# One delta-rule layer of a small transformer on one core: two activation-table switches per stage, a decay mask carried by unused partitions, and another order of the work

## The reference

```python
q = silu(x @ Wq); k = l2norm(silu(x @ Wk)); v = silu(x @ Wv)      # 16 heads of 16
log_f = log_sigmoid(x @ Wf)
gamma = -sigmoid(x @ Wgamma)
a = k * gamma[..., None] * exp(log_f)[..., None]
def step(S, inp):                       # over the 38 tokens of an image
    Sp = S * exp(gk)[..., None]
    u = einsum('bhk,bhkv->bhv', a, Sp) + v
    S = Sp + einsum('bhk,bhv->bhkv', k, u)
    return S, einsum('bhk,bhkv->bhv', q, S)
out = layer_norm(out * sigmoid(x @ Wg1 @ Wg2)) * norm_w @ Wo
```

## Time and profile before

| | us |
|---|---|
| median of 3 runs | 1996.59 (1990.41 to 1997.77) |
| the profiled execution | 1989.77 |
| its span | 1988.0 |
| the stage "ln2" | 21.7 (1281.40 to 1303.05) |
| k = 0, 1, 2 | 18.3, 26.8, 44.2 |
| k = 3 to 7, full | 58.8, 61.7, 58.5, 58.1, 58.1 |
| k = 8, 9, 10 | 56.5, 45.7, 29.7 |

### The profile page before, as it was taken

The page is one execution under the profiler, slowest core; times in us unless marked ns, Lnnn a source line. Parts: engine busy times, 40 slices in busy tenths (PEclk is TensorE's granted clock), DMA queues, the critical chain, the costliest instruction groups (busy, mean ns, idle before and its releaser), DMA issues. The chain is left out here.

```text
span 1988.0 us, 51796 instructions
## 1 busy us (share of the span) xinstructions
PE 1708.2 (86%) x22689; PEld 1517.3 (76%) x22689; DVE 1108.5 (56%) x2379; ACT 656.6 (33%) x1347; POOL 314.5 (16%) x284
## 2 busy tenths in 40 slices
PE   4677786799999999999999999876888888757589
PEld 4466675579988999989999999745877777756468
DVE  3655555674545555455555465566445555543885
ACT  3334534433322233232223232163333333223142
...
DMA packets 10070, 36.01 MB, mean 18 GB/s; under 512 B 3056, under 2 KB 6152, under 8 KB 7304
## 3 DMA queue, kind: packets, MB, share of 16 engines
...
...
## 5 line engine op out<-in xcount | busy, mean ns | idle before, releaser
L1042 ACT ACTIVATE hidden<-bank,moe_b 128x512 f32<-128x512 f32 (+1 forms) x320 | 213.3, 668 | 537.1 <-PE bank L934 524.5
L951 PE MATMUL bank<-moe_w2h,hidden_hi 128*128 128x256 f32 x1216 | 345.7, 284 | 0.0
L951 PE MATMUL bank<-moe_w2l,hidden_hi 128*128 128x256 f32 x1216 | 344.0, 283 | 0.0
L951 PE MATMUL bank<-moe_w2h,hidden_lo 128*128 128x256 f32 x1216 | 343.9, 283 | 0.0
L934 PE MATMUL bank<-x_hi,moe_w1h 128*128 128x512 f32 (+1 forms) x640 | 243.8, 381 | 2.9 <-ACT hidden L1042 2.8
L934 PE MATMUL bank<-x_lo,moe_w1h 128*128 128x512 f32 (+1 forms) x640 | 242.5, 379 | 0.0
L934 PE MATMUL bank<-x_hi,moe_w1l 128*128 128x512 f32 (+1 forms) x640 | 242.0, 378 | 0.0
L951 PEld LDWEIGHTS bank<-moe_w2h,hidden_hi 128*128 128x128 f32 x1216 | 233.1, 192 | 6.0 <-DVE residual L1076 4.3
L1076 DVE SCALAR_TENSOR_TENSOR residual<-bank,gates,residual 128x256 f32<-128x256 f32 x152 | 73.4, 484 | 290.4 <-PE bank L951 290.4
L951 PEld LDWEIGHTS bank<-moe_w2l,hidden_hi 128*128 128x128 f32 x1216 | 233.2, 192 | 1.2
L951 PEld LDWEIGHTS bank<-moe_w2h,hidden_lo 128*128 128x128 f32 x1216 | 233.2, 192 | 0.0
...
## 6 DMA issues: line engine op xcount, KB each, us to landing
...
```

The lines of the kernel that those rows point to most:

```text
L951: mm = nc.tensor.matmul(bank[4 + n % 3][:, 0:D], left, right, start=(i == 0), stop=(i == len(passes) - 1))
L1042: nc.scalar.activation(H[:, i % 4, 0:n], bank[i % 4][:, 0:n], ACT.Relu, bias=b1[:, x, f:f + 1]).then_inc(acted, 1)
```

## The change

On ScalarE a stage loads two table sets in place of three: first that with Sigmoid, under which `forget_parts(p)` and `sigmoid_values(p)` alternate and all sigmoids follow, then that with Ln and Exp, under which `forget_logs` now runs, followed by `padded` and `inverse_norms`. On TensorE projections 0 and 1 stand directly behind the values, `first_half(1)` behind projection 3, the key norms between and behind the remainders, and `inverse_out(0)` and `(1)` ahead of `score(0)` and `(1)`. On VectorE `values_of` stands first, `log_forget` moves behind `with_values(0)`, and the rows of the inverse are laid out otherwise, up to row 15 ahead of `low_out`. On GpSimd both `square` come before `steps`, with `clear_pairs(0)` between.

The mask moves into the free partitions. `here` gets in its free rows a second 0/1 matrix, scaled by 2^30; `after` gets blocks between its halves that pick these rows. The free rows of the log are log_sigmoid(0) = -0.69, so the sum is a large negative number where the mask is wanted. The matmul with `past` goes. The stage "ln2" loads four `from_here` blocks, four blocks of `after` and eight pieces of `free_row`, in place of eight `from_here` blocks.

```diff
--- before.py
+++ after.py
@@ -51,6 +51,7 @@
 MT = 4
 EPS = 1e-5
 MASKED = -1e30
+PAST = 2.0 ** 30
 
 
 @contextmanager
@@ -1220,8 +1221,8 @@
         wg2 = sb(ctx, "delta_wg2", [HD, D])
         same = sb(ctx, "same_head", [P, P])
         after = sb(ctx, "after", [P, P], F32R)
-        past = sb(ctx, "past", [P, SEQ], BF16)
         here = sb(ctx, "from_here", [P, SEQ])
+        free_row = sb(ctx, "free_row", [P, 4])
         emask = sb(ctx, "in_pair", [P, 2])
 
         G1 = sb(ctx, "gate_low", [GATE_ROWS, TOKENS], F32R)
@@ -1244,8 +1245,8 @@
 
             blocks = [(slice(HB * r, HB * r + HALF), slice(PAD * (r // 2) + HALF * (r % 2),
                                                            PAD * (r // 2) + HALF * (r % 2) + HALF)) for r in range(4)]
-            blocks += [(slice(HB * r + HALF, HB * (r + 1)), slice(PAD * (r // 2) + SEQ, PAD * (r // 2) + SEQ + HB - HALF))
-                       for r in range(4)]
+            free = [(slice(HB * r + HALF, HB * (r + 1)), slice((HB - HALF) * r + 1, (HB - HALF) * (r + 1) + 1))
+                    for r in range(4)]
 
             def zero_gate(done):
                 nc.gpsimd.memset(G1[:].bitcast(F32), 0.0).then_inc(done, 1)
@@ -1257,14 +1258,18 @@
                             + [(dst[:], ins[src]) for dst, src in (
                                 (w, "delta_w"), (wg, "delta_wg1"), (wg2, "delta_wg2"),
                                 (nw, "norm_w"), (same, "same_head"))]
-                            + [(here[dst, :], ins["from_here"][src, :]) for dst, src in blocks],
+                            + [(here[dst, :], ins["from_here"][src, :]) for dst, src in blocks]
+                            + [(here[dst, :], ins["after"][src, 0:SEQ]) for dst, src in free]
+                            + [(free_row[dst, 0:2], ins["from_here"][SEQ:SEQ + HALF, SEQ - 2:SEQ])
+                               for dst, src in blocks]
+                            + [(free_row[dst, 0:2], ins["from_here"][0:HB - HALF, SEQ - 2:SEQ]) for dst, src in free],
                             splits=[(wg[:], wgh[:], wgl[:]), (wvf[:], wvfh[:], wvfl[:])]
                             + [(w[:, n], wh[:, i], wl[:, i]) for i, n in enumerate((0, 1, 4))])
 
         with ExitStack() as inner:
             b = delta_buffers(sb, inner, XN)
-            b.update(wh=wh, wl=wl, wvfh=wvfh, wvfl=wvfl, same=same, after=after, past=past, here=here, emask=emask,
-                     ident=ident, identb=identb, XH=XH, XL=XL, xh_c=xh_c, xl_c=xl_c,
+            b.update(wh=wh, wl=wl, wvfh=wvfh, wvfl=wvfl, same=same, after=after, here=here, free_row=free_row, emask=emask,
+                     ident=ident, XH=XH, XL=XL, xh_c=xh_c, xl_c=xl_c,
                      wgh=wgh, wgl=wgl, G1=G1, wg2=wg2, wg2s=wg2s)
             for k in range(CHUNKS + 3):
                 delta_stage(nc, psum, bank, b, k - 1 if 1 <= k <= CHUNKS else None, k if k < CHUNKS else None,
@@ -1411,9 +1416,8 @@
     Q, K, O = range(3)
     (PA, VH, SH, SL, KQ, SQ, KX, SV, GZ, LF, RX, PD, LZ, MS, DS, AS, TT, TS) = (buffers[n] for n in (
         "PA", "VH", "SH", "SL", "KQ", "SQ", "KX", "SV", "GZ", "LF", "RX", "PD", "LZ", "MS", "DS", "AS", "TT", "TS"))
-    (wh, wl, wvfh, wvfl, same, after, past, here, emask, ident, identb, XH, XL, xh_c, xl_c) = (buffers[n] for n in (
-        "wh", "wl", "wvfh", "wvfl", "same", "after", "past", "here", "emask", "ident", "identb", "XH", "XL",
-        "xh_c", "xl_c"))
+    (wh, wl, wvfh, wvfl, same, after, here, free_row, emask, ident, XH, XL, xh_c, xl_c) = (buffers[n] for n in (
+        "wh", "wl", "wvfh", "wvfl", "same", "after", "here", "free_row", "emask", "ident", "XH", "XL", "xh_c", "xl_c"))
     wgh, wgl, G1, wg2, wg2s = (buffers[n] for n in ("wgh", "wgl", "G1", "wg2", "wg2s"))
     NK = KQ
     first = nxt == 0
@@ -1503,12 +1507,10 @@
                     pe.wait_ge(d_exp, b - 1)
                 else:
                     pe.wait_ge(v_out, b + 3)
-                nc.tensor.matmul(bank[4 + b % 2][:, 0:CT], identb[:, :], spread(past[:, :], 1, HPH),
-                                 start=True, stop=False)
                 for part in range(2):
                     mm = nc.tensor.matmul(bank[4 + b % 2][:, 0:CT], after[:, :],
                                           MS[:, b % 2, part].rearrange("p g t -> p (g t)"),
-                                          start=False, stop=(part == 1))
+                                          start=(part == 0), stop=(part == 1))
                 mm.then_inc(d_log, 1)
 
             def score(p):
@@ -1635,34 +1637,34 @@
                 values(p)
             low_part(0)
             low_part(1)
-            first_half(0)
             project(0)
-            first_half(1)
             project(1)
             low_part(2)
-            remainder(0)
+            first_half(0)
             project(2)
             low_part(3)
-            remainder(1)
             project(3)
             low_part(4)
+            first_half(1)
+            remainder(0)
+            key_norm(0)
+            remainder(1)
+            key_norm(1)
             second_half(0)
             decay(0)
             second_half(1)
             decay(1)
-            key_norm(0)
-            key_norm(1)
             output()
             decay(2)
+            inverse_out(0)
             score(0)
             decay(3)
-            inverse_out(0)
+            inverse_out(1)
+            score(1)
             decay(4)
-            score(1)
             decay(5)
-            inverse_out(1)
+            score(2)
             decay(6)
-            score(2)
             decay(7)
             inverse_out(2)
             score(3)
@@ -1773,39 +1775,35 @@
                                          bank[s][:, IP * m * SEQ:IP * (m + 1) * SEQ].rearrange(
                                              "p (i t) -> p i t", t=SEQ), ACT.Copy).then_inc(o_hi, 1)
 
-            nc.scalar.preload_act_table_set("natural_log_exp_and_others")
+            nc.scalar.preload_act_table_set("sigmoid_and_others")
             for p in range(IP):
                 forget_parts(p)
-            forget_logs()
-            nc.scalar.preload_act_table_set("sigmoid_and_others")
-            sigmoid_values(0)
-            sigmoid_values(1)
+                sigmoid_values(p)
+            sigmoid(0)
+            sigmoid(1)
             first_back(0)
-            sigmoid(0)
-            sigmoid_values(2)
-            first_back(1)
-            sigmoid(1)
-            sigmoid_values(3)
-            padded(0)
             sigmoid(2)
-            padded(1)
             sigmoid(3)
             for i in range(len(spans)):
                 low_high(i)
+            first_back(1)
             nc.scalar.preload_act_table_set("natural_log_exp_and_others")
+            forget_logs()
+            padded(0)
+            padded(1)
+            inverse_norms()
             solution(0)
             decay(0)
             solution(1)
             decay(1)
-            inverse_norms()
             high_out(0)
             high_out(1)
             decay(2)
+            inverse_back(0)
             decay(3)
-            inverse_back(0)
+            inverse_back(1)
             decay(4)
             decay(5)
-            inverse_back(1)
             decay(6)
             decay(7)
             inverse_back(2)
@@ -1934,52 +1932,58 @@
             def decay_masks():
                 if not first:
                     return
-                nc.vector.tensor_scalar(past[:, :], here[:, :], 1.0, -MASKED, ALU.subtract,
-                                        ALU.mult).then_inc(masks, 1)
+                nc.vector.tensor_scalar(free_row[:, 2:3], free_row[:, 0:1], -1.0, None, ALU.mult).then_inc(masks, 1)
+                nc.vector.tensor_scalar(free_row[:, 3:4], free_row[:, 0:1], PAST, 1.0, ALU.mult,
+                                        ALU.add).then_inc(masks, 1)
                 dve.wait_ge(zeroed, 1)
                 for s in range(2):
                     nc.vector.tensor_scalar(
                         after[half(s), half(s)].rearrange("p (h s) -> p h s", h=2)[:, :, 0:HALF],
                         here[half(s), :].rearrange("p (h s) -> p h s", h=2), -1.0, 1.0,
                         ALU.mult, ALU.add).then_inc(masks, 1)
+                dve.wait_ge(masks, 1)
+                for s in range(2):
+                    nc.vector.tensor_scalar(
+                        after[half(s), half(1 - s)].rearrange("p (h s) -> p h s", h=2)[:, :, 0:HALF],
+                        here[half(s), :].rearrange("p (h s) -> p h s", h=2), 1.0, free_row[half(s), 2:3],
+                        ALU.subtract, ALU.mult).then_inc(masks, 1)
+                dve.wait_ge(masks, 6)
+                nc.vector.tensor_scalar(here[:, :], here[:, :], free_row[:, 3:4], None, ALU.mult).then_inc(masks, 1)
 
             decay_masks()
             a_out()
             for t in range(1, 5):
                 inverse_row(t)
-            log_forget()
-            inverse_row(5)
+            for p in range(IP):
```

(30 more changed lines are left out.)

## The result

The changed kernel takes 1984.95 us (median of ten executions, 1982.8 to 1987.7) against 1995.45 for the kernel before on the same chips (ten, 1990.4 to 2002.2). The ratio is 0.9949, with a 95% interval of 0.9936 to 0.9962: 10.2 us faster, 7.6 to 12.8 by the interval. The prediction was 13.5 faster, 1983.1. Its total was nearly right, in part by luck: one of its terms was wrong by some 9 us, as the stages show.

The account below looks back on a forecast made before the run. Program fetch was taken to pace the front, VectorE the tail. Full stages -12.5, k=8 -1.7, k=9 -3.6, k=2 -1.9, k=1 +2.3, k=0 +1.0, loads +2.9: -13.5 us, to 1983.1; range 1968 to 1995.

Parts of the forecast that it names:

- step 3: Front of a full stage, counted from its start S: output ends at S+38.4, -0.2 us per stage, bounds -3.3 and +1.
- the fetch's shadow: Full stage's front: projections among small matmuls lie mostly in TensorE's wait for its next program block, at least 3.47 us each.
- Rival B: Full stages' front: the block pace does not hold, so the front gives its 3.3 us; -29 us, 1968; chance 0.15.
- Rival D: Front: output waits for solution(1), behind inverse_norms on ScalarE; about -1 at 3 us lateness, +10 to +12 at 5; chance 0.12.
- Rival C: Tail gains 1.2 instead of 2.3 us, as VectorE meets POOL; block boundary falls badly (+0.6); -5 us, 1992; chance 0.23.
- the signs that were named: Profile after: 22,625 matmuls, full stages 55.5 to 57 us, output's end S+37 to 39.5, issue stops in remainder(0) and output.
- The tail: Behind output() in full stages: rows 11 to 15 move into VectorE's idle time; -2.3 us per stage, bounds -3.5 and -1.2.
- k=8: Stage k=8: same tail without keys, VectorE idles 7.4 us before low_out; gain 1.7 us.
- k=9: Stage k=9: rows 13 to 15 move into VectorE's 8.9 us idle time, last inverse_out follows row 18; -3.6 us.
- k=1: Stage k=1: logs wait for silu 3's sigmoid and the table load, so decay(0) comes later; +2.3 us.
- The loads: Stage ahead of the deltas: eight more small loads on SyncE delay VectorE before prepare; +2.9 us.
- k=0: Stage k=0: seven mask instructions for three on VectorE, both padded ahead of inverse_norms; +1.0 us, bounds 0 and 3.

Follow-up runs that it names:

- new front only: Kernel before with only the order up to output() changed (table switches, projections behind the values, key norms between remainders); mask and tail as before: ratio 1.0031.
- the third of the projections: One of three products of each projection computed: 0.9866 on the kernel before with the new order behind output(), 0.9901 on the kernel after.
- new tail only: Kernel before with only the order behind output() changed (inverse_out ahead of the scores, inverse rows 10 to 15 ahead of low_out): 0.9899, 1971.6 us.
- the second profile: The kernel after run once more with nothing changed, to see how far stages scatter: ratio 0.9951 to the kernel before.
- the mask alone: Kernel before with only the mask in the free rows (64 identity matmuls fewer, eight loads and four VectorE instructions more): ratio 1.0011.
- chain first: Kernel after with first_half(0) ahead of projections 0 and 1 and first_half(1) ahead of 2 and 3 on TensorE: ratio 0.9908.

## Why the prediction was right and where it was wrong

**The front: the step that failed.** In its step 3 the prediction got the output's end at S+38.4 from a chain that starts at S+11.7 and takes 26.7 us. It did charge projections 0 and 1 ahead of the chain (S+10.0 to 11.7), but gave the time back inside: with twelve projection matmuls fewer there, the chain was to be 1.6 us shorter than the 28.3 of before, at 3.47 us for each block. That pace is the closest that k=10 shows, a least time, and the count ("with a boundary at 12.8, next ones at 16.3") took it for every block. It also wrote in its first part that "the projections there lie mostly in the fetch's shadow", and did not draw the conclusion: work taken out of a shadow and set ahead of what casts it is paid in full.

Measured in the five full stages after, the chain starts at S+12.5, 0.8 late, and takes 27.85 us, 1.15 too long: together the 1.9 us by which the front was missed. In k=5 the stops end at S+20.5, 24.4, 31.7, 35.6 and 39.1, where the count has boundaries at 19.7, 23.2, 30.1, 33.6 and 37.1. From the first to the last that is 3.70 us per block, and 3.65 to 3.72 in the other four stages. The 0.8 are the values at the half clock for longer (5.4 us, where new front only, with the same order, has 4.9).

The experiments say the same of the order alone. Taking the projections back behind `first_half(0)` gave 1.6 us per stage and 8 in all; making them a third as long where they stand ahead gave 1.6, and where they lie inside 0.4. Twelve projection matmuls fewer inside did not shorten the chain beyond the scatter: the stops for "issue" grew from 2.7 to 5.5 us instead. Of the term -0.2 x 5 this makes +1.7 x 5 in the profile, 9.5 us off, and it is the only large miss.

Why the 1.75 us ahead were not used to fetch, the packets show: one block at most is loaded beside the one in use, and the next is asked for only when TensorE enters that one. In the five full stages of the kernel after the last packet ahead of the chain starts at S+2.5 to S+6.3 and the next at S+12.8 to S+14.5, after the chain has begun. The rule of the Trainium skill that was cited ("Advanced Engine Details and Errata", ISA Cache: lines of 256 instructions, two of them) says the same. The 128 KB that this section gives for TensorE beside it would be eight such blocks; the packets here show nothing of that depth.

**Rival B** (the front gives 3.3 us) fell, and with it the doubt whether the stops of k=10 hold for full stages: the third of the projections shows them 3.5 to 4.0 us apart there too. **Rival D** (`output` waits for the norms on ScalarE) did not come: `output` of k=5 starts at 1546.46 with no wait, its stops are for "issue". **Rival C** was wrong on the tail; its longer front came, but at 1.9 us above the forecast and not 0.6, and by the pace of all blocks, not by where one boundary fell. Of the signs that were named, the 22,625 matmuls, the stops in `remainder(0)` and `output` and the 17.1 us behind `low_out` came as written; a full stage of 55.5 to 57 us did not (57.4 to 58.8), nor did an output's end by S+39.5 (S+40.3 in the mean).

**The tail** was -2.75 and -3.0 in the two profiles after, for -2.3 predicted, inside its bounds of -3.5 and -1.2; the tail alone has -2.67. It is the rows in VectorE's idle time (1.8) and, as far as the scatter lets one say, the earlier `inverse_out` (0.9); the prediction had given the second no gain ("first `weigh` at T+4.1 (now 3.84 to 4.36: same)"). k=8 was right (-1.7). k=9 gave -2.6 for -3.6: its low parts to the end are 3.6 shorter, as predicted (and from the first `x_hi` on 8.5 instead of 12.1 us in every kernel with the new rows), and its front is 1.0 longer. That front has no projections; all of the 1.0 is in its stops for "issue" (10.0 us after, 9.0 before), and these scatter: the front of k=9 takes 33.0 to 35.7 us in the versions with the new tail, 33.1 to 33.7 in the three without. Whether the new order has a share in it stays open.

**k=1** was +4.1 (and +3.8 in the second profile) for +2.3. The mechanism was right: the logs behind all the sigmoids and a table load. Its size was not: the prediction priced the delay of `decay(0)`, which measures 2.7 us, but the stage is longer by another 1.4 behind it. There the next two `decay` wait 0.6 us each for POOL's `steps`, with none ready ahead, and the stage's granted clock is 0.67, where 0.88 is seen with the old order; the clock alone does not make it, as the 27.25 us of the mask alone at 0.75 show. With the old order in k=0 and k=1 the stage is 25.8 us.

**The loads** cost 1.4 us in the first profile and 2.3 in the second (VectorE waits 3.05 us there), and not 2.9. In the first, of 2.8 us more of issues on SyncE only half reached VectorE: it went on 2.7 us after the last issue before, and 1.1 us after it in the kernel after. With one or two transfers the wait is 0 to 0.22 us, with eight 0.66 to 1.20, with sixteen 2.16 to 3.05, so the issues were what set it, but not all of them stood behind the bulk of the weights. **k=0** +1.3 and +0.75 for +1.0; **k=2** -0.8 and -1.0 for -1.9, inside its bounds.

**The total.** The terms as measured in the first profile are 1.4 + 1.3 + 4.1 - 0.8 + 5 x (1.7 - 2.75) - 1.7 - 2.6 + 0.3 = -3.3, and the stage "ln2" begins 1.5 us earlier in this profile than in that of before: that makes the 4.8 by which the two profiled executions differ. Compared like with like, profile with profile, -13.5 missed by 8.7 us. The medians differ by 10.2 because the kernel before scatters over 12 us and its profiled execution was faster than all ten, while the kernel after scatters over 5. So -13.5 came close to -10.2 by luck: the front was 9.5 us too good, and the profile of before, from which the forecast was worked out, happened to lie 5.7 us under its median. The sum of parts measured by medians (-11.7) is the better account. Where the kernel before spends the 5.7 us in a usual execution is open: no profile of one was taken.

Left open besides: whether the new front really costs +1.7 us a stage with the new tail and only +0.5 (and +0.6 in the tail) with the old one. The chain starts 2.0 us later there too, but is 27.1 us long, the shortest of all, beside a kernel before whose 28.6 are the longest; the three versions with projections 0 and 1 ahead have fronts of 39.1 to 40.35 us, the four with the old front 38.1 to 38.9. And whether k=1's 5 us reach the whole.

The best that these runs point to is the change without its front and mask: `new tail only`, 1971.6 us, by the ratios 10 us faster than the kernel after and 20 faster than before. Versions that add chain first, the old order in k=0 and k=1, and a single load (0.9877 to 0.9895) can't be told from it.
